# A degree histogram on TensorE: which one-hot is loaded and which is moved, with index loads cut into parts of 64 and 3 partitions

## The reference

```
deg  = segment_sum(1, dst) + 1          # how many edges end in each node, plus a loop
dinv = 1 / sqrt(deg)
out  = segment_sum((h @ W)[src] * dinv[src] * dinv[dst], dst) + b      # twice
```

## Time and profile before

| | |
|---|---|
| median of 3 executions | 4023.84 us (4022.74 to 4029.69) |
| profiled execution, first to last instruction | 4021.7 us |
| PE busy | 3225.8 us, 80% |
| DVE busy | 2091.2 us, 52% |
| histogram stage, first transpose to last matmul | 89.3 to 324.8 us |
| granted TensorE clock, mean / in the histogram | 0.872 / 0.50 |

### The profile page before, as it was taken

The page is one execution under the profiler, slowest core; times in us unless marked ns, Lnnn a source line. Parts: engine busy times, 40 slices in busy tenths (PEclk is TensorE's granted clock), DMA queues, the critical chain, the costliest instruction groups (busy, mean ns, idle before and its releaser), DMA issues.

```text
span 4021.7 us, 75601 instructions
## 1 busy us (share of the span) xinstructions
PE 3225.8 (80%) x22339; PEld 2393.9 (60%) x22340; DVE 2091.2 (52%) x4959; ACT 950.7 (24%) x2067; POOL 1600.5 (40%) x1599
## 2 busy tenths in 40 slices
PE   2886677899999999699777777777777878777777
PEld 2772234566666666699555555556555656666666
DVE  6777777888887787544322233333333333333333
ACT  4110012233444444211212111111111111111112
POOL 0000000000000000000777777777777777777774
PEclk7557999999999999899788888888888888888888
DMA  1000001111111221597222222222222222222222
GB/s 54 0 0 0 16 17 48 48 65 79 67 81 81 85 93 81 231 351 273 76 76 74 76 76 74 76 73 76 76 73 76 74 72 76 74 75 76 73 74 62
DMA packets 178797, 324.55 MB, mean 81 GB/s; under 512 B 30987, under 2 KB 138308, under 8 KB 166106
## 3 DMA queue, kind: packets, MB, share of 16 engines
q1 hardware_dynamic: 127482, 217.13, 15.0%
q0 software_dynamic: 51168, 106.07, 10.1%
HBM read 238.00 MB, written 85.09 MB: 80 GB/s over the span
## 4 chain that ended last, share of the span: by engine, by line
PE 36%; POOL 33%; issue 17%; DVE 9%; DVEq 2%; DMA 2%; POOLq 0%; ACT 0%; ACTq 0%; SPq 0%
POOL shared L437 33%; PE pa L1154 9%; PE pb L1154 8%; PE pc L1148 5%; PE pd L1148 4%; PE pd L1113 3%; PE pc L1318 2%; DVE loop_col L873 2%; PE pb L1303 2%; DVE loop_lo L877 1%; DMA shared<-lin_table,idx 1%; DVE c L873 1%; DVE agg L809 1%; DMA shared<-in_src_dram 1%; DVEq L311 1%
## 5 line engine op out<-in xcount | busy, mean ns | idle before, releaser
L437 POOL DMA_INDIRECT shared<-lin_table,idx x1568 | 1585.7, 1011 | 479.0 <-issue 471.7
L466 POOL DMA_DIRECT2D lin_table<-c x12 | 9.2, 770 | 1896.0 <-ACT c L617 1896.0
L1318 PE MATMUL pc<-shared 128*128 128x128 f32 x3904 | 566.2, 307 | 106.7 <-DVE shared L1022 106.7
L1318 PEld LDWEIGHTS pc<-shared 128*128 128x128 f32 x3904 | 548.4, 224 | 116.1 <-DVE shared L1022 116.1
L1303 PE MATMUL pb<-we_sb,shared 128*128 128x128 f32 x3136 | 614.1, 356 | 0.2 <-ACT shared L667 0.2
L667 ACT ACTIVATE shared<-pa,be_col 128x512 f32<-128x512 f32 x392 | 247.8, 683 | 1536.1 <-PE pa L1292 1536.1
L1303 PEld LDWEIGHTS pb<-we_sb,shared 128*128 128x128 f32 x3136 | 520.8, 251 | 120.0 <-issue 106.7
L1027 DVE TENSOR_TENSOR agg<-agg,pc 128x128 f32 x244 | 70.1, 287 | 951.9 <-PE pc L1318 951.9
L1015 DVE TENSOR_TENSOR shared<-pb,shared 128x512 f32<-128x512 f32 x392 | 252.4, 686 | 426.7 <-DMA shared<-lin_table,idx 419.3
L1299 PE MATMUL pb<-be_parts,ones 3*128 3x512 bf16 x392 | 178.0, 454 | 359.1 <-DVE shared L1015 358.9
L873 DVE TENSOR_SCALAR loop_col<-col_h,shared 128x784 bf16<-128x784 f16 x780 | 326.5, 419 | 92.6 <-PE pa L1154 52.4
(11 more groups left out here) (201 smaller groups left out, 3830.8 us busy)
## 6 DMA issues: line engine op xcount, KB each, us to landing
adjacency<-shared SPq DMA_DIRECT2D x49, 1568.0 KB, 5.6
shared<-adjacency SPq DMA_DIRECT2D x49, 1568.0 KB, 8.6
shared<-in_edge_attr_dram SPq DMA_DIRECT2D x195, 256.0 KB
shared<-lin_table,idx POOLq DMA_INDIRECT x1568
lin_table<-c POOLq DMA_DIRECT2D x12, 256.0 KB, 7.1
out_dram<-xr SPq DMA_DIRECT2D x12, 256.0 KB
shared<-in_dst_dram SPq DMA_DIRECT2D x1, 512.0 KB
shared<-in_src_dram SPq DMA_DIRECT2D x1, 512.0 KB
```

Of the source, the lines that this page charges most:

```text
L437: pool.indirect_dma_start(out=dest(s, j), out_offset=None, in_=table, in_offset=bass.IndirectOffsetOnAxis(ap=idx[:, s, j:j + 1], axis=0)). ...
L1318: last = pe.matmul(pc[:, 0:F], hot_f[:, 2 * i + h, :], msg[:, h, i, :], start=(h == 0 and i == 0), stop=(h == 1 and i == 3))
```

## The change

Two edits. In the histogram the operands trade places: the 49-wide `hist_hi` is loaded as weights, the 128-wide `hist_lo` is moved, and the sum is now 49 partitions by 128. It is therefore copied to SBUF and transposed once at the end, before the square root. The layouts of the two tiles stay. In the index loads, the 67-partition transfer becomes one of 64 partitions and one of 3, for `dst` and for `src`, and the two waits for all of them (ACT and DVE) count eight transfers instead of six.

```diff
+EVEN1 = FULL1 // 16 * 16
+        count_sb = sb("count_sb", [NB, P], fp32)
-        deg_ps = pd[:, 0:NB]
+        count_ps = pd[0:NB, 0:P]
+        deg_ps = pc[:, 0:NB]
...
-                sp.dma_start(raw[0:FULL1, 1, :],
-                             arr[P * GE:(P + FULL1) * GE].rearrange("(p e) -> p e", e=GE)).then_inc(raw_loaded, 16)
+                for first, end in ((0, EVEN1), (EVEN1, FULL1)):
+                    sp.dma_start(raw[first:end, 1, :],
+                                 arr[(P + first) * GE:(P + end) * GE].rearrange("(p e) -> p e", e=GE)).then_inc(raw_loaded, 16)
...
-            act.wait_ge(raw_loaded, 16 * 6)
+            act.wait_ge(raw_loaded, 16 * 8)
...
             act.wait_ge(deg_ready, 1)
+            act.activation(count_sb[:, :], count_ps, ACT.Copy).then_inc(count_out, 1)
+            act.wait_ge(deg_turned, 1)
             act.activation(deg_sb[:, :], deg_ps, ACT.Sqrt, bias=1.0).then_inc(deg_ready, 1)
...
-            pe.matmul(deg_ps, zeros_b[:, :], zeros_b[:, 0:NB], start=True, stop=False).then_inc(hist_used, 1)
+            pe.matmul(count_ps, zeros_b[:, 0:NB], zeros_b[:, :], start=True, stop=False).then_inc(hist_used, 1)
...
-                            last = pe.matmul(deg_ps, hist_lo[:, s, :, u], hist_hi[:, s, :, u], start=False, stop=False)
+                            last = pe.matmul(count_ps, hist_hi[:, s, :, u], hist_lo[:, s, :, u], start=False, stop=False)
...
-            pe.matmul(deg_ps, zeros_b[:, :], zeros_b[:, 0:NB], start=False, stop=True).then_inc(deg_ready, 1)
+            pe.matmul(count_ps, zeros_b[:, 0:NB], zeros_b[:, :], start=False, stop=True).then_inc(deg_ready, 1)
+            pe.wait_ge(count_out, 1)
+            pe.transpose(deg_ps, count_sb[:, :], ident[0:NB, 0:NB]).then_inc(deg_turned, 1)
```

More of the change, by code:

```diff
@@ L249, in gnn_kernel @@
         deg_ready = sem("deg_ready")
+        count_out = sem("count_out")
+        deg_turned = sem("deg_turned")
         class Node:
@@ L726, in _ @@
             step(dve.tensor_copy(win_f[:, :], win_i[:, :]))
-            dve.wait_ge(raw_loaded, 16 * 6)
+            dve.wait_ge(raw_loaded, 16 * 8)
             dve.tensor_copy(raw_f[:, :, :], raw_d[:, :, :]).then_inc(raw_fp, 1)
```

## The result

The changed kernel takes 4168.97 us (4161.73 to 4171.26, 4 runs) against 4023.68 (4 runs of before): a ratio of 1.0351, 95% interval 1.0334 to 1.0368, 145.3 us slower. Forecast were 4155 us, 4100 to 4190, and slower with 0.84.

A forecast was written before the change was run, and what follows sets the result against it. The two-buffer ring with PE's matmuls bound the histogram, a one-engine index load the front. Terms -21.9 (loads), +152.2 (stage) and +0.9 (turn) made +131.2 us: 4152.9 on the profile, 4155 us on the median, range 4100 to 4190.

The forecast's parts named there:

- Index loads: Before the histogram: 67-partition transfers use one of sixteen engines; split ones spread, so DVE starts at 11.5 us, gaining 21.9 us.
- Price of a matmul: Histogram: start-to-start after the swap between 206 and 246 ns, middle 226, against 94 ns before.
- Both readings of the rows: Histogram: the moved operand, not the load, sets the 94 ns; its 16-byte step is slow, 1.92 ns a column.
- The bound changes hands: Histogram: the two-buffer ring binds before, 2.13 us a round; afterwards PE is full and DVE waits over 200 us.
- Stage: Histogram with layer norm: 387.7 us against 235.5, +152.2 us, of which 354.4 us are the 1568 matmuls.
- the layer-norm one: PE's transposes and half-products within the histogram stage, no longer partly covered: 4.5 x 7 = 31.3 us.
- Turn: End of the histogram: copy and transpose of the sum, uncovered, +0.9 us (0.7 to 1.5).
- rival 3: Histogram: a partial price of 130 to 200 ns a matmul, say 165; total 4059 us; chance 0.04.
- Rival 1: Histogram: moved columns cost only the clock, the ring still binds; total 4018.5 us; chance 0.08.
- rival 2: Histogram: as rival 1, and more moved columns raise the clock to 2.4 GHz; total 3956 us; chance 0.06.
- Rival 4: Index loads: the 64-partition transfer doesn't spread, nothing is won in front; total 4177 us; chance 0.02.
- The rule on lines: Moved operand: an access to a new 16-byte line each time pays, two hits a line are wanted; no price given.

The follow-up runs named there:

- experiment 5: Kernel before with one operand read side by side, output not the histogram: 49 moved columns, 66 ns between starts; 128 loaded columns, 90 ns; both strided, 94 ns.
- experiment 2: Changed kernel with its 128 moved columns read side by side, output not the histogram: 94 ns between starts, stage 225 us instead of 396.
- experiment 3: Changed kernel with moved columns 8 or 4 bytes apart instead of 16, output not the histogram: 8 bytes 120 ns (median 117 to 118), 4 bytes as side by side.
- experiment 4: Changed kernel with added matmuls of 512 contiguous columns that hold the clock at 1.00: 228 ns median between the histogram's starts, 377 us of added work.

## Why the prediction was right, point by point

- **Index loads.** -21.9 forecast, -20.8 at DVE and -21.1 at PE's first transpose. The one-engine reading held: with 64 partitions the busy share is 1 where it was 0.06. The rate was overrated, 205, 258 and 160 GB/s instead of 250 all along. `x` came at 24.77 instead of 22.5 us, still well inside its 7 us of cover.
- **Price of a matmul.** 226 ns forecast as the middle of 206 and 246, 228 measured: 1568 x 2.4 ns = 4 us of the miss. Both readings of the rows held: in experiment 5 the move sets before's pace, in experiment 2 the price goes with the step. The fixed part is smaller than the 26 ns of the lower bound and larger than the 0 of the upper; from 94 and 228 ns for 49 and 128 columns it is 94 - 49 x 1.70 = 11 ns, and from the 90 ns of experiment 5, whose load is contiguous, 4 ns at 1.75 a column, next to the 6 and 1.73 of experiment 3. Neither bound had it right; that their middle came within 3 ns is in part luck. The load of 49 strided columns stayed hidden, as forecast.
- **The bound changes hands.** DVE waits 202 us ("over 200" forecast), PE idles 1.4 us.
- **Stage.** 387.7 forecast, 395.9 measured. Beside the 4 us above, the term mis-sized is the layer-norm one, 31.3 us (its own figures add up to 31.5), which counted streams and no change between them: after 58 matmuls the product starts at 97.05 where 83.69 + 58 x 0.228 is 96.91, and the histogram resumes at 100.22 where 97.05 + 14 x 0.212 is 100.02. Some 0.3 us at each of 14 places are 4 us.
- **Turn.** 0.9 forecast, 0.7 measured.
- **Total.** The profiled span is 4169.6 us where 4152.9 was forecast, 16.7 more: 0.8 in front, 8.2 in the stage, -0.2 in the turn, and 7.9 behind the square root, where the forecast had a mere shift and where no cause is shown.
- **Rivals.** Clock-priced columns (1 and 2) are refuted by the 228 ns, and by experiment 4 at the high clock; so is the partial price of rival 3. Rival 1 names L1148 among the f32 streams; its row is bf16. The mechanism of rival 2, a clock that rises, is seen in experiment 2, where 128 moved columns side by side go with 0.95 and the same number with a step of 16 bytes with 0.50; it would not have given its 3956 us, since the starts stay 91 ns apart and the ring holds the stage. Rival 4 is refuted by the front.
- **The rule on lines.** The 228 ns and the 8 bytes' 117 agree in direction with what the prediction took from the Trainium skill, "SBUF — State Buffer", section "Door 1: The DMA port swizzle". That two hits a line are enough for full bandwidth, as the Trainium skill says there, the 8-byte step does not bear out: 118 ns at a granted clock of 1.00, where columns side by side took 91, and 118 at 0.50, where they took 107.

## What to carry to other kernels

Before two operands of a matmul trade places, look at the step of the one that will be moved: with bf16 columns 16 bytes apart a column costs 1.7 ns at either clock (228 ns for 128), and a wider moved side multiplies that. The sign in the profile is a start-to-start time well over columns by clock, while a load that is known to be cheap does not bring the next start forward. And read the chain for one round first: here neither engine was full, so two more buffers gave 49 us in the stage, where matmuls a third cheaper (66 ns instead of 94, experiment 5) gave 23.

## What the runs showed of the hardware that was not expected

- Loading 49 strided bf16 columns seems no cheaper than loading 128: in experiment 2 matmuls at the high clock follow each other every 91 to 94 ns though the moved side is contiguous; with 128 loaded strided columns (before, moved side flat) it was 62 to 66 ns at the low clock. The number of loaded columns fell by 2.6 and the price rose. The 49 columns at the moved side's 1.73 ns, and 6, would be 91 ns too, but the 128 do not follow that. That the load is what holds these starts is inferred, as said above.
- A single matmul of 128 moved columns 16 bytes apart has a duration of 407 ns at a granted clock of 0.50 and at 1.00 alike.
- Writing one DVE loop for four groups a turn instead of two shortened a later, unchanged stage by 15 us of 1288, and DVE's waits of no visible cause in it from 119.9 to 104.1 us.
